# A Mamba-2 mixer with a gated expert FFN on one core: the end of the program reordered, with early returns of gate and input

## What is computed

```python
xn = layernorm(x)
proj = xn @ in_proj_w.T                       # gate 8192, xBC 10240, dt 128
xBC = silu(conv1d_causal(xBC, conv_w) + conv_b)
y = ssd(x, B, C, D, softplus(dt + dt_bias))   # chunked scan, 128 heads of 64, 8 groups
yg = y * silu(gate)
s = (yg * rsqrt(mean(yg**2 within a group) + eps)) * norm_w @ out_proj_w.T
g = silu(top2_of_16_experts(xn))              # the FFN
out = x + s * g
```

## Time and profile before

| | us |
|---|---|
| median of 3 runs | 1733.6 (1731.6 to 1734.77) |
| the profiled execution, its own time | 1733.94 |
| its span | 1731.8 |
| TensorE busy in it | 1670.0 (96%) |
| VectorE busy in it | 1492.6 (86%) |

### The profile page before, as it was taken

How to read it: one execution, slowest core, us unless ns; L and a number is a source line. 1 busy time by engine, 2 the same in 40 slices (tenths; PEclk the granted TensorE clock), 3 DMA queues, 4 the chain that set the end, 5 groups by cost and what they waited for, 6 DMA issues and landing times.

```text
span 1731.8 us, 31320 instructions
## 1 busy us (share of the span) xinstructions
PE 1670.0 (96%) x9236; PEld 1307.0 (75%) x9236; DVE 1492.6 (86%) x1729; ACT 1028.1 (59%) x1601; POOL 924.9 (53%) x593
## 2 busy tenths in 40 slices
PE   7699989999999999999999999999999999999996
PEld 5477867777777777777777777777777777777775
DVE  6533698898999899998999899989999899989996
ACT  4233476666666667666666666566666666665751
POOL 3442265555565555565565556555655555555652
PEclk9799999999999999999999999999999999999999
DMA  3332222212221122122222222222221222122204
GB/s 120 111 96 69 76 76 71 65 52 66 76 66 52 64 78 71 58 58 64 79 64 57 59 72 69 60 59 71 77 59 46 76 72 62 61 60 74 70 21 146
DMA packets 73458, 121.39 MB, mean 70 GB/s; under 512 B 12366, under 2 KB 17870, under 8 KB 73252
## 3 DMA queue, kind: packets, MB, share of 16 engines
q1 hardware_dynamic: 72676, 117.92, 22.7%
q10 hardware_dynamic: 576, 1.05, 0.2%
HBM read 112.64 MB, written 6.29 MB: 69 GB/s over the span
## 4 chain that ended last, share of the span: by engine, by line
PE 73%; DVE 15%; issue 7%; ACT 2%; POOL 1%; DMA 1%; DVEq 0%; SPq 0%; ACTq 0%; POOLq 0%
PE pj L455 13%; PE pj L457 12%; PE pj L456 12%; PE sc L625 6%; PE ob L455 6%; PE ob L456 5%; PE ob L457 5%; DVE conv L1229 3%; PE seg L604 3%; PE tb L614 3%; PE sc L629 3%; DVE wo_lo L1293 2%; DVE decay L1257 2%; DVE xc L1243 1%; DVE yT_lo L1285 1%
## 5 line engine op out<-in xcount | busy, mean ns | idle before, releaser
L966 POOL TENSOR_TENSOR w_lo<-stg,w_hi 128x512 fp32r<-128x512 f32 x316 | 514.3, 1628 | 430.4 <-ACT w_hi L832 335.8
L455 PE MATMUL pj<-xT_hi,w_hi 128*128 128x512 f32 x1208 | 480.8, 398 | 7.6 <-DVE conv L1229 5.1
L456 PE MATMUL pj<-xT_lo,w_hi 128*128 128x512 f32 x1208 | 472.1, 391 | 0.0
L457 PE MATMUL pj<-xT_hi,w_lo 128*128 128x512 f32 x1208 | 472.1, 391 | 0.0
L1229 DVE SCALAR_TENSOR_TENSOR conv<-pj,par,conv 128x510 f32<-128x510 f32 (+2 forms) x480 | 357.2, 744 | 60.1 <-ACT conv L840 47.8
L996 POOL TENSOR_TENSOR xc<-xc,thg 128x512 f32<-128x512 f32 x128 | 202.5, 1582 | 259.8 <-DVE xc L1280 259.8
L1257 DVE TENSOR_TENSOR decay<-decay,gm 128x1536 f32<-128x1536 f32 x128 | 282.7, 2209 | 0.0
L455 PEld LDWEIGHTS pj<-xT_hi,w_hi 128*128 128x128 f32 x1208 | 227.3, 188 | 66.6 <-DVE conv L1229 8.1
L457 PEld LDWEIGHTS pj<-xT_hi,w_lo 128*128 128x128 f32 x1208 | 227.3, 188 | 49.1
L456 PEld LDWEIGHTS pj<-xT_lo,w_hi 128*128 128x128 f32 x1208 | 227.5, 188 | 45.1
L455 PE MATMUL ob<-wo_hi,yT_hi 128*128 128x512 f32 x540 | 223.3, 414 | 7.4 <-DVE part L1306 4.9
(11 more groups left out here) (169 smaller groups left out, 2270.6 us busy)
## 6 DMA issues: line engine op xcount, KB each, us to landing
stg<-wstream SPq DMA_DIRECT2D x387, 256.0 KB, 2.7
rowt<-cs_scr SPq DMA_DIRECT2D x384, 4.0 KB
colt<-cs_scr SPq DMA_DIRECT2D x384, 4.0 KB
acc<-hid SPq DMA_DIRECT2D x8, 256.0 KB, 4.7
decay<-gate_scr SPq DMA_DIRECT2D x8, 256.0 KB, 4.1
xc<-hid SPq DMA_DIRECT2D x8, 256.0 KB, 5.4
out<-acc SPq DMA_DIRECT2D x8, 256.0 KB, 2.0
gate_scr<-part SPq DMA_DIRECT2D x4, 256.0 KB, 2.0
```

Of the source, the lines that this page charges most:

```text
L455: nc.tensor.matmul(dst, hi_w, hi_x, start=first, stop=False)
L456: nc.tensor.matmul(dst, hi_w, lo_x, start=False, stop=False)
L457: return nc.tensor.matmul(dst, lo_w, hi_x, start=False, stop=last)
L966: nc.gpsimd.tensor_tensor(w_dest(n, 1), stg[:, s % RING, :], f32(w_dest(n, 0)), ALU.subtract).then_inc(S["wl"], 1)
```

## The change

- **Banks.** In the last half, `out_first` of tiles 0 to 3 writes a bank of its own for each tile (`ob` and the three banks of `seg`), and leaves the sum there. Tile 1's block, the first in `seg`, waits for the last `exp`. The other pairs are added in the same banks: at the end pairs 4 to 6 of each tile (9 matmuls a tile), with `square_sums` behind tile 1, and then pair 7 of each tile (3 matmuls). `keep_first` and `add_second` are gone for this half.
- **Returns.** SyncE's queue returns gate and input of tiles 0 to 3 as soon as the last weights are split, into `bc`, `conv` and the weight ring `stg`, and those of tiles 4 to 7 into `part` and `decay` as these come free. Each tile has a semaphore of its own.
- **Finishing.** `finish` of all 8 tiles (now: acc of the second half holds only the other 7 groups) stands on VectorE in front of step 7, behind it, and around `y_lo` and `mean_square`. What is left per tile 4+t is `finish_last`: bank * rstd * gate, then acc = 0.5 * that + acc.

```diff
+FINISH = [0, 1, 2, 4, 3, 5, 6, 7]
...
+        gate_t = [bc[:, 0, :], bc[:, 1, :], conv[:, 0, :], conv[:, 1, :]] + [part[:, t, :] for t in range(4)]
+        flat = [decay[:, n].rearrange("p q c -> p (q c)") for n in range(NDEC)]
+        hid_t = [stg[:, t, :] for t in range(4)] + [flat[2][:, H * t:H * (t + 1)] for t in range(3)] + [flat[0][:, 0:H]]
+        last_bank = [ob[:, :], seg[:, 0, :], seg[:, 1, :], seg[:, 2, :]]
...
-            sp.wait_ge(S["y"], at(G, 0, NJ, 0))
-            for i in range(NTT):
-                nc.sync.dma_start(gate_t[:, i, :], gate_scr[i * P:(i + 1) * P, :]).then_inc(S["gre"], 16)
-            sp.wait_ge(S["sq"], at(G, 0, NJ, 0))
-            sp.wait_ge(S["ylo"], at(G, 0, NJ, 0))
-            for i in range(NTT):
-                nc.sync.dma_start(xc[:, i, :], hid[i * P:(i + 1) * P, :]).then_inc(S["xre"], 16)
-            for n, i in enumerate((0, 4, 1, 5, 2, 6, 3, 7)):
-                sp.wait_ge(S["fin"], 2 * n + 2)
+            def back(i):
+                nc.sync.dma_start(gate_t[i], gate_scr[i * P:(i + 1) * P, :]).then_inc(s_back[i], 16)
+                nc.sync.dma_start(hid_t[i], hid[i * P:(i + 1) * P, :]).then_inc(s_back[i], 16)
+            sp.wait_ge(S["bcp"], at(G - 1, 1, 1, 1))
+            sp.wait_ge(S["silu"], at(G - 1, 1, NX, NX))
+            sp.wait_ge(S["wl"], index(G - 1, 1, LAST[-1]) + 1)
+            sp.wait_ge(S["ol"], oindex(G - 1, NJ))
+            for t in range(4):
+                back(t)
+            for t in range(4):
+                sp.wait_ge(S["acc"], at(G - 1, 0, 4, 4 + t + 1))
+                sp.wait_ge(S["y"], at(G - 1, 1, NJ, 6 if t < 3 else 7))
+                back(4 + t)
+            for n, i in enumerate(FINISH):
+                if i < 4:
+                    sp.wait_ge(S["fin"], 2 * n + 2)
+                    nc.sync.dma_start(out[i * P:(i + 1) * P, :], acc[:, i, :]).then_inc(S["outs"], 16)
+            for t in range(4):
+                sp.wait_ge(S["out"], 2 * t + 2)
+                i = 4 + t
                 nc.sync.dma_start(out[i * P:(i + 1) * P, :], acc[:, i, :]).then_inc(S["outs"], 16)
...
+                if is_last(g, half):
+                    if t == 1:
+                        pe.wait_ge(S["exp"], at(G, 0, NJ, 0))
+                    out_last(t, range(4))
+                    return
...
+            def out_last(t, pairs):
+                for k in pairs:
+                    mm = product(last_bank[t], yT_hi[:, k, t * P:(t + 1) * P], yT_lo[:, k, t * P:(t + 1) * P],
+                                 wo_hi[:, k, :], wo_lo[:, k, :], k == 0, k == NJ - 1)
+                if pairs[-1] == NJ - 1:
+                    mm.then_inc(S["o"], 1)
...
             out_of_step(G, 0, 0)
-            square_sums(G, 0)
-            for s in range(1, 5):
-                out_of_step(G, 0, s)
+            pe.wait_ge(S["ylo"], at(G - 1, 1, NJ, NJ - 1))
+            for t in range(4):
+                out_last(t, range(4, NJ - 1))
+                if t == 1:
+                    square_sums(G, 0)
+            pe.wait_ge(S["ylo"], at(G, 0, NJ, 0))
+            for t in range(4):
+                out_last(t, range(NJ - 1, NJ))
...
+            def finish_last(t):
+                i = 4 + t
+                dve.wait_ge(S["o"], at(G - 1, 1, NJ, t + 1))
+                dve.wait_ge(S["rs"], at(G - 1, 1, 1, 1))
+                nc.vector.scalar_tensor_tensor(out=gate_t[i], in0=last_bank[t], scalar=rstd[:, t:t + 1], in1=gate_t[i],
+                                               op0=ALU.mult, op1=ALU.mult).then_inc(S["out"], 1)
+                dve.wait_ge(S["out"], 2 * t + 1)
+                nc.vector.scalar_tensor_tensor(out=acc[:, i, :], in0=gate_t[i], scalar=0.5, in1=acc[:, i, :],
+                                               op0=ALU.mult, op1=ALU.add).then_inc(S["out"], 1)
```

More of the change, by code:

```diff
@@ L228, in build @@
             wh wl oh ol pr cps tap conv tanh silu bcp gm segs drop exp w xt xdt y u tg sg yg yhi sq sa ylo
-            msp ms rs o pa pb acc fin xre gre outs""".split()
+            msp ms rs o pa pb acc fin out outs""".split()
         S = {n: sem("s_" + n) for n in names}
@@ L233, in build @@
         s_gout = [sem(f"s_gout{i}") for i in range(4)]
+        s_back = [sem(f"s_back{i}") for i in range(NTT)]
         s_dt = [sem(f"s_dt{i}") for i in range(2)]
@@ L308, in build @@
         iota = rt[:, 496:512]
-        gate_t = decay[:, :, :, :].rearrange("p r q c -> p (r q c)")[:, 0:NTT * H].rearrange("p (t c) -> p t c", t=NTT)
+        gate_t = [bc[:, 0, :], bc[:, 1, :], conv[:, 0, :], conv[:, 1, :]] + [part[:, t, :] for t in range(4)]
+        flat = [decay[:, n].rearrange("p q c -> p (q c)") for n in range(NDEC)]
+        hid_t = [stg[:, t, :] for t in range(4)] + [flat[2][:, H * t:H * (t + 1)] for t in range(3)] + [flat[0][:, 0:H]]
+        last_bank = [ob[:, :], seg[:, 0, :], seg[:, 1, :], seg[:, 2, :]]
         @block.sync
@@ L884, in out_of_step @@
                 before = (g, 0) if half == 1 else (g - 1, 1)
-                if s >= 6:
+                if s >= 6 and not is_last(g, half):
                     keep_first(g, half, s - 6)
@@ L949, in _ @@
             square(G - 1, 1, NJ - 1)
-            out_of_step(G, 0, 0)
-            out_of_step(G, 0, 1)
         @block.gpsimd
@@ L1351, in step, with finish @@
                     x_silu(*of_half(g, half, m), m)
-            def finish(i, n):
-                dve.wait_ge(S["gre"], 16 * NTT)
-                nc.vector.scalar_tensor_tensor(out=acc[:, i, :], in0=acc[:, i, :], scalar=0.5, in1=gate_t[:, i, :],
+            def finish(n):
+                i = FINISH[n]
+                dve.wait_ge(s_back[i], 2 * 16)
+                dve.wait_ge(S["acc"], at(G - 1, 0, 4, 4 + 4))
+                nc.vector.scalar_tensor_tensor(out=acc[:, i, :], in0=acc[:, i, :], scalar=0.5, in1=gate_t[i],
                                                op0=ALU.mult, op1=ALU.mult).then_inc(S["fin"], 1)
                 dve.wait_ge(S["fin"], 2 * n + 1)
-                dve.wait_ge(S["xre"], 16 * NTT)
-                nc.vector.tensor_tensor(acc[:, i, :], acc[:, i, :], xc[:, i, :], ALU.add).then_inc(S["fin"], 1)
+                nc.vector.tensor_tensor(acc[:, i, :], acc[:, i, :], hid_t[i], ALU.add).then_inc(S["fin"], 1)
+            def finish_last(t):
[7 more added lines that the diff above has]
+                                               op0=ALU.mult, op1=ALU.add).then_inc(S["out"], 1)
             for s in range(4, NJ):
@@ L1374, in _ @@
             step(G - 1, 0, 7)
-            for s in range(NJ):
+            for s in range(7):
                 step(G - 1, 1, s)
+            finish(0)
+            finish(1)
+            step(G - 1, 1, 7)
+            finish(2)
+            finish(3)
             y_lo(G - 1, 1, NJ - 1)
+            finish(4)
+            finish(5)
             mean_square(G - 1, 1)
+            finish(6)
+            finish(7)
             for t in range(4):
[L1380 to L1384, removed]
+                finish_last(t)
 def kernel(**inputs):
```

## The result

The changed kernel takes 1722.31 us in the median of 6 runs (1721.04 to 1725.37), the kernel before 1733.44 us (6 runs, 1731.6 to 1734.77). The ratio is 0.9938, 95% interval 0.9927 to 0.9949: faster, by 0.6%, 8.8 to 12.7 us. The forecast was 1725.1 us, in a range of 1722.7 to 1728.3. The profiled execution took 1722.46 us with a span of 1720.3.

A forecast was written before the change was run, and what follows sets the result against it. The prediction took the end to be bound by bank `ob`, late loads and VectorE's last instructions. VectorE ending at 1720.8 instead of 1729.35 saves 8.55 us: 1733.94 becomes 1725.4, median 1725.1 us, range 1722.7 to 1728.3.

The forecast's parts named there:

- the 7.6 us: TensorE's end: stalls ahead of the last blocks vanish, 0.15+0.59+6.48+0.4, so the last matmul starts at 1716.7 instead of 1724.34.
- a start after a scan costs 0.17 anyway: TensorE's blocks after scans: 0.17 us idle stays, so those at 1692.08 and 1700.03 gain only 0.15 and 0.59.
- the finishes in the gap ahead of step 7: VectorE: two tiles' finishes, 2.7 us, go where it rests between 1696.4 and 1699.3.
- the turns with GpSimd: VectorE and GpSimd alternate on two-SBUF-operand instructions; pair 7's low part ends at 1707.2, 3.3 us later, costing TensorE nothing.
- four pairs behind the first whole tile: VectorE's end: product from the bank and addition for four tiles, 5.68 us, from 1715.1 to 1720.8.
- the last store: End of the program: stays 2.45 us behind VectorE's end, of which 2.0 is the store itself.
- My 5.4 us for a load: Early returns of gate and input: each lands in 5.4 us, tiles 0 to 3 by 1689.2, first use 1696.5.
- a bound of -0.4 for the start cost: Range's lower side: starts after scans on TensorE may cost nothing, taking 0.4 us off the forecast time.
- Starvation of GpSimd: Rival 1: VectorE's finishes keep the port, TensorE stands 1.5 us at the square sums; 1726.6 us, chance 13%.
- Stalls that only move to the `ylo` waits: Rival 2: TensorE stands 5 us or more at the two `ylo` waits together; about 1731 us, chance 5%.
- A load that holds up step 7: Rival 3: VectorE waits for tile 0's loads ahead of step 7, TensorE stands 3 us, clock falls; 1739 us, chance 2%.
- three owners: The end's bounds in turn: the one bank `ob`, the late loads, and 24 VectorE instructions behind the last products.

The follow-up runs named there:

- the last experiment: Changed kernel with tiles made whole further apart, plus add_second ahead of the gate instruction in steps 2 to 5 of the last half: ratio 0.9929 (0.9915 to 0.9942).

## Why the prediction was wrong

**Where the difference lies.** The sum was made for the profiled execution: 1725.4 us forecast, 1722.46 measured, 2.9 less. Of these, 0.8 lie behind the mark, where the change acts (9.4 us gained there, 8.55 forecast), and 2.1 ahead of it, where the mark came earlier.

**TensorE.** The term that was too small is the 7.6 us by which TensorE's last matmul should come earlier: it measured 8.4 (72.9 against 81.3 from the mark). The step that failed in it: "a start after a scan costs 0.17 anyway". I had read the row at 1683.44, labelled issue, as a fixed cost, and as a block that has nothing to wait for. It waits for VectorE's `add_second`, the reader of the bank, which in that profile ended about when the scan did:

```profile
1682.66 0.68 DVE L1306 TENSOR_TENSOR part<-part,ob 128x512 f32<-128x512 f32 x1
```

Its end, 1683.34, lies 0.10 us ahead of the block's start, and the same 0.10 returns in the second profile of the kernel before (1681.59 and 1681.69). The changed kernel shows the same start with 0.21 and the true releaser, the blocks in fresh banks with no bracket at all, and the last experiment removed it by moving the reader. So the two blocks after scans gained 0.41 and 0.83, not 0.15 and 0.59: 0.5 us. The other 0.3 lies behind the third block's start, from where 17.2 us pass to the last matmul and my terms left 24.31-6.88 = 17.4. The step from the square sums to the next block is 0.08 shorter (0.81 after 0.89), and the matmuls follow each other a little more closely; neither was a term of the sum, and why they do so is open.

**VectorE.** Every step held: the finishes in the gap ahead of step 7, the turns with GpSimd, four pairs behind the first whole tile (forecast 5.68, measured 1717.88-1712.24 = 5.64), the last store 2.4 behind. The low part of pair 7 was even earlier than my 1707.2: on the clock of that forecast it ended at 1704.37+2.1 = 1706.5. Its end lay 7.0 us ahead of TensorE's need (forecast 6.8). VectorE's own end moved by TensorE's 0.8 more: 9.4 against 8.55 in the profile that the sum was made against.

**Loads.** They were never late, as forecast. My 5.4 us for a load was a median; the last of the inputs took 6.96. It cost nothing, as all had more than that to spare. But I took the old wait of 1.60 us for a fixed part of the kernel before. It is 0 to 1.6, which makes the change's own worth 7.8 to 9.4 us. That the mean of it, 8.6, agrees with my 8.55 is luck: the term of TensorE was 0.8 too small, and the profile that I worked from was the one with the longest wait, 0.8 above the mean of three.

**The median and the range.** Over the 11 runs of the change the mean is 1723.1, over the kernel before's 24 it is 1733.2: 10.1 us, with some 1.5 us of scatter in each single run. Of the 10.1 the end explains 8.6 (7.8 to 9.4). The rest is not explained: no part ahead of the mark is touched, and the mark's place scatters in both kernels, by 2.8 us in three profiles of the kernel before, part of it with the granted clock. The falls of the clock come about as often with the change as without it, as far as the runs' mean granted clock tells: it was 0.992 or more in 6 of its 11 runs and in 8 of the 18 of the kernel before that list it. Compared within these two classes the difference is 10.3 and 9.4 us, so their mixture does not account for the rest. The range's lower end, 1722.7, came from a bound of -0.4 for the start cost, where 0.5 was gained, and 2 us of scatter. For the pace it had a bound upward only. With the 0.8 in place of the 0.4 it would have been 1722.3, just at the median of six runs; a second set of five gave 1723.58, inside. So the step above moved the time out of the range, but most of the distance from 1725.1 is scatter and the unexplained rest.

**The rivals.** Starvation of GpSimd: not with four instructions in a row and not with twelve. Stalls that only move to the `ylo` waits: no bracket there. A load that holds up step 7: the first eight were issued by 1675.1 and the slowest took 5.5 us, so they landed some 14 us ahead of use. Which of the "three owners" mattered was not asked in the forecast and turned out the more instructive question: the banks alone 0 to 1.3 us, loads and first-half finishes 2.6 to 4.2, and 5.9 lost of the whole without the place of the finishes.

## What to carry to other kernels

At the end of a program, count what the last engine must still do behind the last product, and move everything that doesn't depend on it into that engine's earlier gaps; faster products alone gave 0 to 1.3 us here, because 20 instructions stood behind them. Then let results become whole at the pace at which their reader takes them (here the last two tiles 2.7 us apart), not all at once: that was another 2 us. A short idle time labelled issue ahead of an instruction that also has a semaphore to wait for may be that wait; the end of the instruction that sets the semaphore, or the same start on an unshared buffer, tells.

## What was unexpected of the hardware

The same 16 loads of 256 KB made VectorE wait for 1.60, 0 and 1.00 us in three profiles of one kernel. The last of them was issued 8.4, 7.9 and 8.1 us behind the first and took 6.96, at most 5.9 and 6.67 us to land, so both the issuing and the landing vary. And the granted clock falls to the 1.2 GHz level for some 3 us near 112 and 265 us in some executions and not in others. TensorE stands still for 2.6 and 2.4 us just ahead of these places, with the fall and without it, so such a stand does not decide by itself. One fall moves everything behind by some 1.5 us, a seventh of what the change brings.
